# A two-layer graph network on one core: thirteen node tiles summed by gathered rows instead of eleven

## What is computed

```python
h = relu(layernorm(x))
agg = segment_sum(edge_attr, dst) / max(count, 1)           # edges x 64
x = x + relu(concat(agg, h) @ W1 + b1) @ W2 + b2            # layer 0
h = relu(layernorm(x))
summed = segment_sum(h[src], dst) / max(deg, 1)             # layer 1
x = x + h @ w_self.T + b_self + summed @ w_neigh.T
```

## Time and profile before

| what | value |
|---|---|
| median of three runs | 1150.4 us (1147.02 to 1151.46) |
| span of the profiled execution | 1162.0 us; a time of its own is not given beside it |
| TensorE busy | 1093.1 us, 94% |
| GpSimd busy | 531.4 us, 46% |
| DVE busy | 788.8 us, 68% |
| ACT busy | 491.8 us, 42% |
| mean granted TensorE clock | 0.982 |
| data moved by DMA | 131.93 MB |

### The profile page before, as it was taken

One profiled execution on the slowest core, in us unless ns is written; L12 is line 12 of the kernel. 1 busy time (PEld: TensorE's weight loads), 2 busy tenths in 40 slices (PEclk: granted clock), 3 DMA queues, 4 the chain that ended last, 5 costly groups with the idle time before them and its releaser, 6 DMA issues.

```text
span 1162.0 us, 29643 instructions
## 1 busy us (share of the span) xinstructions
PE 1093.1 (94%) x11380; PEld 792.0 (68%) x11380; DVE 788.8 (68%) x1849; ACT 491.8 (42%) x957; POOL 531.4 (46%) x502
## 2 busy tenths in 40 slices
PE   3789999999999997899989999999999999999998
PEld 2667777777777775566666666676666666666665
DVE  6777878887864768665656666666666666666662
ACT  5445636333114464444343444444444444444441
POOL 3010111110003662676566666766667666667620
PEclk9799999999999999899999999999999999999999
DMA  8766655555561220233223233333333333333310
GB/s 259 215 210 202 191 159 163 163 156 162 174 220 46 73 74 27 73 98 90 87 81 89 87 96 94 89 92 91 91 96 92 88 99 89 93 90 96 95 35 19
DMA packets 72618, 131.93 MB, mean 114 GB/s; under 512 B 12414, under 2 KB 32594, under 8 KB 72492
## 3 DMA queue, kind: packets, MB, share of 16 engines
q1 hardware_dynamic: 51820, 75.25, 20.9%
q0 software_dynamic: 20672, 55.00, 16.6%
HBM read 117.25 MB, written 12.95 MB: 112 GB/s over the span
## 4 chain that ended last, share of the span: by engine, by line
PE 85%; DVE 7%; issue 2%; DVEq 2%; ACT 2%; DMA 2%; another core or an unknown queue 1%; ACTq 0%; SPq 0%
PE bank L1214 33%; PE couples L1207 10%; PE couples L1037 9%; PE bank L1233 7%; PE bank L982 7%; PE bank L994 6%; PE bank L1245 3%; PE bank L976 2%; PE bank L1225 2%; PE couples L1042 2%; DVE oreg L1645 1%; PE couples L947 1%; DMA kreg<-in_edge_attr_dram 1%; PE couples L982 1%; DVE oreg L1394 1%
## 5 line engine op out<-in xcount | busy, mean ns | idle before, releaser
L1214 PE MATMUL bank<-hreg,areg 128*128 128x512 f16 x1862 | 458.8, 384 | 0.0
L627 POOL DMA_INDIRECT wide<-h_table,aggn x332 | 363.9, 1096 | 202.7 <-PE couples L1207 122.0
L845 ACT ACTIVATE areg<-couples 128x784 bf16<-128x784 f32 x304 | 249.3, 823 | 380.3 <-PE couples L1207 336.5
L1214 PEld LDWEIGHTS bank<-hreg,areg 128*128 128x128 bf16 x1862 | 240.4, 144 | 96.0 <-issue 2.6
L1645 DVE TENSOR_TENSOR hids<-iota,kreg 128x1024 bf16<-128x1024 f16 (+1 forms) x304 | 177.5, 625 | 134.2 <-PE couples L1207 123.3
L1645 DVE TENSOR_TENSOR oreg<-iota,kreg 128x1024 bf16<-128x1024 f16 (+1 forms) x304 | 177.4, 625 | 39.2 <-PE couples L1207 29.5
L1037 PEld LDWEIGHTS couples<-oreg,kreg 128*64 128x64 f32 x3232 | 119.0, 144 | 65.2 <-issue 64.1
L1037 PE MATMUL couples<-oreg,kreg 128*64 128x48 f32 x3232 | 140.4, 232 | 21.5 <-DVE oreg L1394 17.5
L595 POOL TENSOR_TENSOR xr<-xr,b2bc 128x512 f32 x25 | 33.6, 1342 | 223.4 <-ACT h0buf L717 223.4
L1394 DVE TENSOR_TENSOR oreg<-iota,wide 128x384 f32<-128x384 f32 x202 | 122.9, 609 | 4.4 <-issue 1.3
L994 PE MATMUL bank<-wide,hids 128*128 128x256 f32 x400 | 104.2, 398 | 0.0
(11 more groups left out here) (176 smaller groups left out, 1117.4 us busy)
## 6 DMA issues: line engine op xcount, KB each, us to landing
kreg<-in_edge_attr_dram SPq DMA_DIRECT2D x202, 256.0 KB, 2.8
h_table<-hreg SPq DMA_DIRECT2D x25, 256.0 KB
xr<-in_x_dram SPq DMA_DIRECT2D x6, 1024.0 KB, 6.9
wide<-h_table,aggn POOLq DMA_INDIRECT x332
out_dram<-hbuf SPq DMA_DIRECT2D x38, 128.0 KB
out_dram<-h0buf SPq DMA_DIRECT2D x10, 128.0 KB
wide<-in_L_gnn_W_dram SPq DMA_DIRECT2D x2, 512.0 KB, 8.9
hids<-h_table,aggn POOLq DMA_INDIRECT x64
```

The lines of the kernel that those rows point to most:

```text
L627: pool.indirect_dma_start(near_rows(n % RING, w), None, table, bass.IndirectOffsetOnAxis(ap=nearsrc[:, k:k + 1], axis=0)).then_inc(s_rows[ ...
L845: act.activation(step.rearrange("p (a k) -> p a k", a=2), cpl[s % 2][:, :, 0:BC * KEYS], ACT.Copy).then_inc(s_adj, 1)
L1214: ins = pe.matmul(bank[4 + par], adj[:, par, :, h], htab[:, h, :], start=(h == 0), stop=(h == TN - 1))
```

## The change

Two more tiles go by index: GB is 7, `TWICE` 4, so DT is 36 and GT 13. Seven fetches are planned in four steps. The products of a tile by index go to bank 6 (the one in which its transposes stood, copied out by then), and DVE reads its result there. The first quad of the next tile by index waits for DVE's scaling (`s_sumN`) instead of its result (`s_res`) and may come in step 5 of the dense tile in which the tile before ends. The transposes that follow a tile by index wait for that tile's result; the others wait as before, for ACT's copy. The number of fetches rises from 396 to 468, that of quads from 99 to 117, that of steps falls from 304 to 288.

```diff
@@ -88,8 +88,8 @@
-    GB = 6
-    TWICE = 2
+    GB = 7
+    TWICE = 4
     DB = 20
     DT = 2 * DB - TWICE
     GT = TN - DT
@@ -105,12 +105,12 @@
-    PACE = 7, 5
+    PACE = 7, 4
     LANDED = 3
     fetch_step = [k * PACE[1] // PACE[0] for k in range(GT * GC * WS)]
     quad_step, finish = [], []
     for g in range(GT):
-        free = (finish[-1] + 1) * ST + 2 if finish else 0
+        free = finish[-1] * ST + 5 if finish else 0
@@ -1218,7 +1218,9 @@
-                if later(m):
+                if m > 0 and order[m - 1] >= DT:
+                    pe.wait_ge(s_res, m)
+                elif m > 0:
                     pe.wait_ge(s_trs, m)
@@ -1238,7 +1240,7 @@
                 if c == 0 and n > 0:
-                    pe.wait_ge(s_res, place[DT + n // GC - 1] + 1)
+                    pe.wait_ge(s_sumN, place[DT + n // GC - 1] + 1)
@@ -1282,7 +1284,7 @@
                             if s == 5:
                                 transposes(place[DT + g])
                             if s == 6:
-                                products(place[DT + g], bank[7])
+                                products(place[DT + g], bank[6])
@@ -1651,7 +1653,8 @@
                 dve.wait_ge(s_near, 16 * 2 * GB)
-                late = [spare[0:GR, b * SL:(b + 1) * SL] for b in range(GB - 2)] + [unreached[0:GR, 0:SL], layer1[0:GR, 0:SL]]
+                late = [spare[0:GR, b * SL:(b + 1) * SL] for b in range(GB - 3)] + [
+                    unreached[0:GR, 0:SL], layer1[0:GR, 0:SL], layer1[0:GR, SL:2 * SL]]
@@ -1755,7 +1758,7 @@
                         for g in ended:
                             if s == 0:
-                                result(DT + g, place[DT + g], 2, g or None, bank[7])
+                                result(DT + g, place[DT + g], 2, g or None, bank[6])
```

## The result

The changed kernel takes 1152.64 us (median of 20 runs), the kernel before 1149.77 in its 20: ratio 1.0025, interval 1.0014 to 1.0037. It is a little slower, by a quarter of a per cent, where 1.2% faster was forecast. A second batch gave 1.0026 (1.0011 to 1.004) from nine runs of the changed kernel; a tenth took 1528.8 us at a granted clock of 0.655 and is left out of that ratio.

What follows compares the result with a forecast made beforehand. TensorE, busy 94% of the 1162.0 us span, was taken to bound: -19.3 + 3.3 + 2.0 = -14.0 gives a span of 1148.0; less the 11.6 between span and median, 1136.4 us, range 1130.5 to 1149.

Steps and rivals of the forecast that it cites:

- What TensorE loses: TensorE in layer 1: two dense tiles go (27.2 us less), 18 quads come (7.9 more); net 19.3 us less.
- ahead of layer 1: DVE's near_in and near_out before layer 1 grow and delay its start by 2.0 us; bounds 0.9 and 4.0.
- waits for rows: TensorE's quads sometimes wait locally for GpSimd's fetched rows: 3.3 us taken, bounds nothing and 8.3.
- the forecast's floor of 17: TensorE bounding all the way, with few waits for rows: -19.3 + 2.0 = -17.3 us, 1133.1.
- What GpSimd gains in work: GpSimd in layer 1: 468 fetches instead of 396, each 1.33 us with its gap; bounds 1.30 and 1.396.
- Rival 3: GpSimd's fetches lock into DVE's one-hots; at a price of 1.396 the time is 1161.5 us; chance 0.11.
- Who comes last: End of layer 1: last fetch needed by 1097.6, GpSimd done at 1095.1, so TensorE sets the end.
- the chain that was called unbroken: Profiled chain of waits in layer 1: each piece starts where the last ended, so its length is its price.
- I carry the difference over: Final sum: the profiled span is 11.6 us longer than the median run, so 11.6 comes off the forecast span.
- Rival 2: GpSimd bounds layer 1 at 1.35 us a fetch: span 1153.0, time 1141.4 us; chance 0.20.
- At nothing: Products in bank 6, the first quad's wait for scaling, DVE's one-hots and SyncE's stores: taken to add no time.
- rival 4: At tile ends DVE's result comes late and transposes wait: one us at each of 13 gives 1149.4; chance 0.05.

Runs made afterwards that it cites:

- third batch's profile: The kernel before, unchanged, profiled again beside the repeats without late signals: 1149.96 us, span 1148.2.
- first batch: Kernel before, unchanged, at 1162.29 us; beside it the changed kernel with six fetches left out 1.0562, with 37 left out 1.0286, and twelve tiles by index 1.0176.

## Why the prediction was wrong

**What TensorE loses: right.** The term was 19.3 us. With half the one-hots, where GpSimd hardly bounds, the time fell by 19.0, of which 2.8 are shorter waits of the couples for DVE (6.6 us instead of 9.4). The rest is 16.2, where 19.3 less the 0.7 ahead of layer 1 and the 1.4 of waits for rows is 17.2; within the 1 us that is left over, the forecast's floor of 17 fits.

**What GpSimd gains in work: right in kind, too small in size.** The price of a fetch was taken as 1.33 and measured 1.349 and 1.357: 468 x 0.019 to 0.027 = 9 to 13 us. The row nearest to "never waits" seemed to be the third and later fetches of an unbroken row (0.03 less); the mean of all that followed at once (1.35) was the right one. The 137 fetches that averaged 1.03 were third or later behind one that had waited; counted with that one, third or later are 208, and they average 1.047, nearly the 1.049 measured. My guess is that those late in a row lie where TensorE's steps are long, while a GpSimd that never waits also runs through the short ones; nothing here tests it. Rival 3's lock, three fetches at 1.37, did not last: the mean with its gap, 1.349 and 1.357, stayed below 1.396.

**Who comes last: the step that failed.** The prediction had TensorE set the end and GpSimd just keep up ("on the whole that just suffices"). The sum set two times against each other: GpSimd's, 468 times its own price from a fixed start, and TensorE's, the last quad at 1118.4. The second came from an execution with late signals in it, and stood 14 us later than in the third batch's profile (1.3 of them ahead of layer 1); the first has none. A delay of TensorE's signals makes TensorE look as if it left GpSimd more time. With the last quad of the third batch's profile the same sum reads: 1104.4 - 19.3 + 0.7 = 1085.8, minus 1.9 for the landing, so the last fetch would have to end by 1083.9; GpSimd ends at 468.4 + 468 x 1.349 = 1099.7 by the product, and at 1101.8 in the profile. It is 16 to 18 us late, and the whole gain of 17 is gone.

The prediction's own terms could have shown it. From layer 1's first couples to the last quad the kernel before has 286 steps' couples, 1751 dense products, 45 tiles' ends and 98 quads, by those terms 626 us. The third batch's profile has 636.7 there (467.75 to 1104.42), of which 6.6 are waits of the couples for DVE; the one that the prediction read has 649.3 (469.08 to 1118.37). After the change the same terms give 607 us, less than the 622 that GpSimd needs even at 1.33. And the chain that was called unbroken has 4.47 us at 540.62 that the profile gives to no engine.

**"I carry the difference over": the same fault at the end.** The 11.6 us between the span and the median were taken from every case alike. A sum that starts from a span with late signals needs that; the sum of a GpSimd that never waits has no such delay in it, and nothing to take off. Rival 2, at 1.35, named the right bound and gave a span of 1153.0; measured were 1147.5 and 1151.0. Left as it stood and with 1.8 around it, it would have been 1154.8, within half a per cent of no change. It was given 1141.4, and a chance of 0.20. Its 3.5 for the landing was too much by 1.6. The sign of the fault was even in the text (the timed runs may lack the stops), and was priced at a part of 3.3 us instead of 14.

**Right by luck.** The forecast's span, 1148.0, and its last quad, about 1104, stand beside 1147.5 and 1103.7 in the profile. They agree because two faults cancel: the late signals that the sum started from (14 us) are gone, and waits for rows (13.7) and for DVE stand in their place. Only the time, from which the signals had been taken off a second time, shows the miss.

**Waits for rows: 3.3 taken (bound 8.3), 13.7 and 17.2 measured.** This is the shortfall above, seen from TensorE.

**Ahead of layer 1: 2.0 taken, 0.7 measured.** From the first fetch of the lists by index to the first couples of layer 1 it is 42.45 us in the kernel before of the third batch (425.30 to 467.75) and 43.15 in the changed one (423.60 to 466.75). Near_in did wait for the lists and near_out did grow:

```profile
444.49 0.87 DVE L1660 TENSOR_SCALAR h0buf<-iota,gshift 72x128 f32<-72x128 f16 x4 [1.12 <-DMA wide<-in_src_dram,gstart]
...
459.37 0.86 DVE L1683 SCALAR_TENSOR_TENSOR noplace<-cntN,noplace 128x1 f32<-128x1 f32 x4
```

DVE stood 1.12 us for the lists (0 to 2.5 foreseen), and L1680, here L1683, runs four times. The wait was covered by DVE's later idle time; near_out's part was not: from the fifth one-hots to the sixth 6.03 us (454.32 to 460.35) instead of 5.22.

**At nothing: nearly.** The transposes never waited for DVE's result, so rival 4 was no danger. The bank edits did cost some 3 us with eleven tiles; 2.2 of that are longer waits for DVE's one-hots, and no quad or transpose waits for the bank. Together with the shortfall this makes the small loss. From layer 1's first couples to the end of the span there are 680.45 us before and 680.75 in the first profile of the changed kernel: 19.3 less work, 13.7 more waits for rows, 3.3 more waits for DVE (12.7 after 9.4), and 2.6 that I can't place. The second profile, of an execution nearer the median, has 683.9: 17.2 of waits for rows, and 2.3 not placed.

**One-hots and fetches.** In the changed kernel's trace 79 fetches ran beside no one-hot of DVE at all and average 0.948 us. Those that started with about 0.2 us of a one-hot left average 1.01 (138), with 0.4 left 1.20 (42), with 0.6 left 1.375 (60); the 19 in its last 0.1 us average 1.07, as the next one-hot is close. The 129 that started just ahead of a one-hot, with none under way, average 0.96. So a fetch is held by what is left of the one instruction that runs when it starts, less some 0.15 us. In the prediction's row that is what happened: the first of the two one-hots ended 0.46 after the fetch had started, and the delay was 0.32; the 0.94 that the prediction set against it is what was left of the pair. The Trainium skill (SBUF — State Buffer, the warning on DVE blocking DMA) says that a DVE instruction that holds the shared port pair keeps GpSimd from writing its descriptors. Half the one-hots agree that DVE delays a fetch: 0.982 instead of 1.049. The page ties its warning to DVE's 2-port modes. The one-hots are `tensor_tensor`, which by the same page has none, contends only with GpSimd's reads, and did not stall a DMA in its probe; here the measurement decides. In the prediction the rule spoke against the change, and rightly; what the sum needed was the price over all phases.

## What to carry to other kernels

When work is moved from the engine that bounds to one that runs beside it, compare the two rates and not the busy shares: here 7 fetches x 1.35 = 9.4 us against four steps of TensorE, 9.0 (17.3 and 19.5 for eight, by the prediction's own terms, 18.1 on average over 36 tiles with 13 ends). Before two engines' finishing times are compared, check that the execution read is an ordinary one (its span against the timed runs) and find which engine the excess belongs to; an excess must not be subtracted from a case that another engine bounds. And take the smaller step when the bound is near: twelve tiles gave 0.5%, thirteen nothing.

## What the runs showed of the hardware

A fetch of 128 rows cost GpSimd 0.948 us on average beside no one-hot of DVE and up to 1.5 beside them (two of 2.0 and 2.2 in the run of the bank edits), with 0.30 of gap in any case; its rows were there 1.8 to 1.9 us after it ended (18 of the 20 quads that waited for rows in the first profile of the changed kernel started at that distance). In the first profile of the kernel before ACT's copies started up to 2.2 us later behind their couples than the usual 0.57, and in the first batch up to 6.4 (six fewer, 871.59 to 878.55); in the profiles of the other two batches none did, nor in the first one of the changed kernel. The changed kernel with six fetches fewer cost 65.6 us against the kernel before in the first batch, and gained 6.4 in the second.
